# A macaron layer on one core: the work between the last mixed chunk and the first paired chunks, in another order and other banks

## The reference

```python
x = x + 0.5 * ffn(layernorm(x)); x = x + mixer(layernorm(x)); x = x + 0.5 * ffn(layernorm(x))
# ffn: x = fwht(x * SU_ug) / 64;  h = silu(x @ W_gate.T * s1) * (x @ W_up.T * s2)
#      fwht(h * SU_dp) / 64 @ W_down.T * s3                      (512 -> 2048 -> 512)
# mixer: y = ssd(...) * silu(gate); y = y * rsqrt(mean(y*y) + eps) * norm_w; y @ out_proj_w.T
```

## Time and profile before

| what | value |
|---|---|
| runs | 1649.05 us median of 3 (1648.89 to 1649.43) |
| the profiled execution | 1650.64 us, its span 1648.9 us |
| busy | TensorE 98%, VectorE 66%, ScalarE 40%, GpSimd 28% of the span |
| mean granted clock of TensorE | 0.995 |

### The profile page before, as it was taken

The page is one execution under the profiler, slowest core; times in us unless marked ns, Lnnn a source line. Parts: engine busy times, 40 slices in busy tenths (PEclk is TensorE's granted clock), DMA queues, the critical chain, the costliest instruction groups (busy, mean ns, idle before and its releaser), DMA issues.

```text
span 1648.9 us, 25148 instructions
## 1 busy us (share of the span) xinstructions
PE 1615.0 (98%) x9612; PEld 1304.5 (79%) x9612; DVE 1087.8 (66%) x2096; ACT 660.8 (40%) x988; POOL 459.6 (28%) x365
## 2 busy tenths in 40 slices
PE   7999999999999999999999999999999999899999
PEld 4788888878888778888778888877888877678887
DVE  7544445675677777777776768777775775665543
ACT  5334343464433463333454333355333341343321
POOL 1666662012212212212212222222131221543400
PEclk9999999999999999999999999999999999999999
DMA  7855555654454444454444444445444435432334
GB/s 285 303 201 206 215 192 204 230 182 153 159 167 163 137 160 152 152 171 144 154 163 149 157 165 152 158 146 183 146 166 162 161 106 178 141 128 90 128 101 155
DMA packets 230886, 274.76 MB, mean 167 GB/s; under 512 B 14064, under 2 KB 190320, under 8 KB 222192
## 3 DMA queue, kind: packets, MB, share of 16 engines
q1 hardware_dynamic: 230768, 273.15, 49.3%
HBM read 222.79 MB, written 50.33 MB: 166 GB/s over the span
## 4 chain that ended last, share of the span: by engine, by line
PE 69%; DVE 5%; ACT 2%; issue 2%; DMA 1%; POOL 1%; SPq 0%; ACTq 0%; DVEq 0%; POOLq 0%
PE bank L1263 23%; PE bank L1219 12%; PE bank L1306 10%; PE bank L1431 5%; PE bank L1343 5%; PE bank L1320 3%; PE bank L1500 3%; PE bank L1471 2%; PE bank L1487 2%; PE bank L1449 2%; PE bank L1494 1%; PE bank L1459 1%; DMA cum_stay<-m_aS 1%; DVE res L2044 1%; DVE xT L2018 0%
## 5 line engine op out<-in xcount | busy, mean ns | idle before, releaser
L1263 PE MATMUL bank<-fxT,wj 128*128 128x512 f32 x1608 | 381.5, 390 | 0.0
L1263 PEld LDWEIGHTS bank<-fxT,wj 128*128 128x128 f32 x1608 | 301.6, 188 | 62.8
L1219 PE MATMUL bank<-xT,wi 128*128 128x512 f32 x900 | 225.8, 399 | 1.5 <-DVE m_cv L2127 0.5
L1306 PE MATMUL bank<-m_wd,m_hb 128*128 128x512 f32 x864 | 218.0, 395 | 3.6 <-DVE res L2044 2.7
L1219 PEld LDWEIGHTS bank<-xT,wi 128*128 128x128 f32 x900 | 168.2, 190 | 40.3 <-issue 5.0
L1306 PEld LDWEIGHTS bank<-m_wd,m_hb 128*128 128x128 f32 x864 | 161.1, 189 | 37.9 <-DVE res L2044 3.8
L1734 ACT CAST m_hb<-xn 128x512 fp32r<-128x512 f32 x76 | 47.1, 620 | 342.8 <-DVE xn L2031 334.9
L2492 POOL TENSOR_TENSOR m_L<-m_L,m_GT 128x512 f32<-128x512 f32 x36 | 52.7, 1463 | 436.7 <-ACT m_L L1788 436.7
L2044 DVE TENSOR_TENSOR res<-bank,res 128x512 f32<-128x512 f32 x148 | 101.9, 689 | 34.6 <-PE bank L1306 32.5
L1788 ACT ACTIVATE m_L<-bank 128x512 f32<-128x512 f32 x128 | 76.5, 598 | 86.8 <-PE bank L1449 86.5
L2031 DVE SCALAR_TENSOR_TENSOR xn<-bank,sc,xn 128x512 f32<-128x512 f32 x76 | 56.7, 746 | 68.1 <-PE bank L1263 68.0
(11 more groups left out here) (279 smaller groups left out, 2742.0 us busy)
## 6 DMA issues: line engine op xcount, KB each, us to landing
wj<-ug_split SPq DMA_DIRECT2D x155, 512.0 KB, 4.2
m_wd<-dn_split SPq DMA_DIRECT2D x43, 1024.0 KB, 4.9
wi<-in_split SPq DMA_DIRECT2D x76, 512.0 KB, 3.3
ug_split<-b_wu SPq DMA_DIRECT2D x8, 2048.0 KB, 14.2
m_wo<-out_split SPq DMA_DIRECT2D x32, 512.0 KB, 4.1
in_split<-b_msp SPq DMA_DIRECT2D x20, 512.0 KB, 3.8
wi<-ug_split SPq DMA_DIRECT2D x17, 512.0 KB, 4.2
raw<-in_wug SPq DMA_DIRECT2D x8, 1024.0 KB, 6.9
```

Of the source, the lines that this page charges most:

```text
L1219: ins = pe.matmul(to[:], w[:, a, k, :], xT[:, b, k, :], start=(k == 0 and i == 0), stop=(k == KH - 1 and i == 2))
L1263: ins = pe.matmul(to[:], w[:, a, k, :], frm[:, b, k, :], start=(k == 0 and i == 0), stop=(k == KH - 1 and i == 2))
L1306: ins = pe.matmul(F[t % 2][:], hb[:, a, j, ck(t)], w[:, b, j, :], start=(j == 0 and n == 0), stop=(j == 1 and n == 2))
```

## The change

- The last output projection writes its four groups to banks 1, 3, 2 and 5 (`last_out_bank`) instead of 6 and 7 in turn, and waits for the last readers of those banks.
- The down product of chunk 33 writes to banks 6, 7, 0 and 1 (`down_bank`), and the gate and up products of chunk 34 wait for two additions less.
- On VectorE the small operations of the root stand behind the four additions of chunk 32's down product, instead of ahead of them.
- On TensorE the turns of the last sequence stand behind chunk 33's second up product; ScalarE and VectorE follow.
- Sums of rows 2 and 3 and the low part of 2 are made by VectorE (`third_difference`, `fourth_difference`, `sums_of_rows_low`); GpSimd keeps `sums_of_weights`. The low parts of all four are done before the first unit, in the order 1, 0, 2, 3 (`SPLIT`), and ScalarE rounds all four ahead of the hidden rows of chunk 34.

```diff
     PRODUCTS = 7
+    SPLIT = (1, 0, 2, 3)
+    SUMMED = (TPG, TPG, TPG + 1, TPG + 4)
+    SPLIT_UP = (TPG + 3, TPG + 2, TPG + 5, TPG + 6)
     order = [BI_DT, BI_B, BI_C] + [i for b in range(NB) for i in (NB + b, b)]
...
 
+        def down_bank(at, t):
+
+            return (F[0], F[1], PB, A)[t] if at == MIXED + 1 else F[t % 2]
+
+        def last_out_bank(t):
+
+            return (A, X, Y, S[1])[t]
+
         def ending_bank(t):
...
                 if x == 0:
-                    sp.wait_ge(s_tp, TPG + 2)
+                    sp.wait_ge(s_tv, SUMMED[3])
                 elif x <= PAIRED + 1:
...
 
-            def up0(at, pairs=0):
-                wait(pe, s_acc, downs(at) - 1)
-                wait(pe, s_oa, TPG * pairs)
+            def up0(at):
+                wait(pe, s_acc, downs(at) - (3 if at == MIXED + 2 else 1))
                 half_up(4 * place_of(at) + 1, F[0]).then_inc(s_u, 1)
...
                 if not opens(at):
-                    pe.wait_ge(s_acc, downs(at))
+                    pe.wait_ge(s_acc, downs(at) - (2 if at == MIXED + 2 else 0))
                 pe.wait_ge(s_sil, 2 * at + 1)
...
                     pe.wait_ge(s_sil, 2 * at + 2 if closes(at) else 2 * at + 3)
-                else:
+                elif at != MIXED + 1:
                     pe.wait_ge(s_acc, downs(at) + t - 1)
+                elif t == 2:
+                    pe.wait_ge(s_pev, LGATE * BATCH)
+                else:
+                    pe.wait_ge(s_oa, TPG * NPAIR * BATCH)
                 for j in range(2):
                     for n, (a, b) in enumerate(PASSES):
-                        ins = pe.matmul(F[t % 2][:], hb[:, a, j, ck(t)], w[:, b, j, :], start=(j == 0 and n == 0), stop=(j == 1 and n == 2))
+                        ins = pe.matmul(down_bank(at, t)[:], hb[:, a, j, ck(t)], w[:, b, j, :], start=(j == 0 and n == 0), stop=(j == 1 and n == 2))
                 ins.then_inc(s_d, 1)
...
                 else:
-                    pe.wait_ge(s_L, QUADS * MIXED)
+                    pe.wait_ge(s_acc, TPG * (MIXED + 2))
                 product(x_bank, a11, b11, True)
...
                 pe.wait_ge(s_sl, u + 1)
-                pe.wait_ge(s_tv, TPG + 2)
+                pe.wait_ge(s_tv, SPLIT_UP[1])
                 pe.wait_ge(s_sn, 4 * u + 1)
...
                 pe.wait_ge(s_cc, 3 * u + 1)
+                pe.wait_ge(s_tv, SPLIT_UP[0])
                 product(y_bank, s1, t1, True)
                 part(1 if u else 3)
-                pe.wait_ge(s_tp, TPG + 3)
+                pe.wait_ge(s_tv, SPLIT_UP[2])
                 pe.wait_ge(s_sn, 4 * u + 2)
...
                 pe.wait_ge(u_loaded, u_count)
-                pe.wait_ge(s_tv, TPG + 3)
+                pe.wait_ge(s_tv, SPLIT_UP[3])
                 pe.wait_ge(s_sn, 4 * u + 4)
...
                 pe.wait_ge(s_yl, 2 * (pair + 1))
+                if pair == NPAIR * BATCH - 1:
+                    pe.wait_ge(s_L, QUADS * MIXED)
+                    pe.wait_ge(s_ex, MIXED)
+                    pe.wait_ge(s_y, MIXED)
+                    pe.wait_ge(s_st, MIXED)
                 for t in range(TPG):
-                    if t >= 2:
+                    if pair == NPAIR * BATCH - 1:
+                        to = last_out_bank(t)
+                    else:
+                        to = F[1 - t % 2]
+                    if pair == NPAIR * BATCH - 1:
+                        pass
+                    elif t >= 2:
                         pe.wait_ge(s_oa, TPG * pair + t - 1)
-                    elif pair == NPAIR * BATCH - 1:
-                        pe.wait_ge(s_acc, downs(at) - t)
                     elif t == 0:
...
                         for n, (a, b) in enumerate(PASSES):
-                            ins = pe.matmul(F[1 - t % 2][:], yh[:, (2 * pair + i) % 4, a, ck(t)], wout[i][:, b, :],
+                            ins = pe.matmul(to[:], yh[:, (2 * pair + i) % 4, a, ck(t)], wout[i][:, b, :],
                                             start=(i == 0 and n == 0), stop=(i == 1 and n == 2))
...
                     out_proj(NPAIR * BATCH - 1, at)
-                up0(at, NPAIR * BATCH if at == MIXED else 0)
+                up0(at)
                 gate1(at)
-                if at == MIXED + SOLO - 2:
+                up1(at)
+                if at == MIXED + 1:
                     for t in range(TPG):
                         beside_turn(ITEMS - 1, t)
-                up1(at)
                 if at < MIXED + SOLO - 1:
...
                 else:
-                    act.wait_ge(s_tv, TPG + 3)
-                    act.wait_ge(s_tp, TPG + 3)
+                    act.wait_ge(s_tv, SPLIT_UP[3])
                 act.copy(pair_hidden(p, g)[:, 0, j, :], four(u)[:, g, :]).then_inc(s_hh, 1)
...
 
-                if i < 2:
-                    act.wait_ge(s_tv, TPG)
-                else:
-                    act.wait_ge(s_tp, TPG + i - 1)
+                act.wait_ge(s_tv, SUMMED[i])
                 act.copy(tb[:, 0, i], tf[:, i]).then_inc(s_th, 1)
...
             hidden_high(at, 0)
+            silu(at, 1)
             for t in range(TPG):
                 beside_row(ITEMS - 1, t)
-            silu(at, 1)
             for t in range(TPG):
...
             silu(at, 0)
-            sums_of_rows_high(0)
-            sums_of_rows_high(1)
-            sums_of_rows_high(2)
+            for i in SPLIT:
+                sums_of_rows_high(i)
             hidden_high(at, 0)
-            silu(at, 1)
             sums_of_weights_high(0)
+            silu(at, 1)
             hidden_high(at, 1)
...
                 paired_silu(u, 0)
-                if u == 0:
-                    sums_of_rows_high(3)
                 snapshot(u, 3, 4, y_bank)
...
                 dve.wait_ge(s_d, downs(at) + t + 1)
-                frm = end_bank(t) if at == LAST - 1 else F[t % 2]
+                frm = end_bank(t) if at == LAST - 1 else down_bank(at, t)
                 dve.tensor_tensor(r, frm[:], r, ALU.add).then_inc(s_acc, 1)
...
 
+            def third_difference():
+                dve.wait_ge(s_tv, TPG)
+                dve.tensor_tensor(tf[:, 2], tf[:, 1], bf[:, 0:2], ALU.subtract).then_inc(s_tv, 1)
+
+            def fourth_difference():
+                dve.wait_ge(s_tv, TPG)
+                dve.tensor_tensor(tf[:, 3], bf[:, 2:4], tf[:, 1], ALU.subtract).then_inc(s_tv, 1)
+
             def sums_of_rows_low(i):
 
-                dve.wait_ge(s_th, i + 1)
+                dve.wait_ge(s_th, 1 + SPLIT.index(i))
                 dve.tensor_tensor(tb[:, 1, i], tf[:, i], tb[:, 0, i].bitcast(F32), ALU.subtract).then_inc(s_tv, 1)
...
                 dve.wait_ge(s_op, TPG * pair + t + 1)
+                frm = last_out_bank(t) if pair == NPAIR * BATCH - 1 else F[1 - t % 2]
                 if pair % NPAIR:
-                    dve.tensor_tensor(acc[:, t, :], F[1 - t % 2][:], acc[:, t, :], ALU.add).then_inc(s_oa, 1)
+                    dve.tensor_tensor(acc[:, t, :], frm[:], acc[:, t, :], ALU.add).then_inc(s_oa, 1)
                 else:
-                    dve.tensor_copy(acc[:, t, :], F[1 - t % 2][:]).then_inc(s_oa, 1)
+                    dve.tensor_copy(acc[:, t, :], frm[:]).then_inc(s_oa, 1)
 
...
             next(other)
-            next(other)
             at = MIXED + 1
...
             next(other)
-            bias(1, s_fs)
             hidden(at, 0)
+            next(other)
+            bias(1, s_fs)
             hidden_low(at, 0)
+            hidden(at, 1)
             for t in range(TPG):
                 beside_turn(ITEMS - 1, t)
-            row_differences(0)
-            hidden(at, 1)
             hidden_low(at, 1)
-            at = MIXED + 2
             for t in range(TPG):
-                add_down(at - 1, t)
-                if t < TPG - 1:
-                    row_differences(t + 1)
-            sums_of_rows_low(0)
+                row_differences(t)
+            at = MIXED + 2
+            add_down(at - 1, 0)
+            add_down(at - 1, 1)
+            third_difference()
+            add_down(at - 1, 2)
             sums_of_rows_low(1)
+            add_down(at - 1, 3)
+            sums_of_rows_low(0)
+            fourth_difference()
             hidden(at, 0)
             hidden_low(at, 0)
-            hidden(at, 1)
+            sums_of_rows_low(2)
+            sums_of_rows_low(3)
             sums_of_weights_low(0)
+            hidden(at, 1)
             hidden_low(at, 1)
...
                     part(3)
-                    sums_of_rows_low(3)
                 second_up(u)
...
                 pool.tensor_tensor(bf[:, k], xT[:, 0, k].bitcast(F32), xT[:, 1, k].bitcast(F32), ALU.add).then_inc(s_tp, 1)
-            pool.wait_ge(s_tp, TPG)
-            pool.wait_ge(s_tv, TPG)
-            pool.tensor_tensor(tf[:, 2], tf[:, 1], bf[:, 0:2], ALU.subtract).then_inc(s_tp, 1)
-            sums_of_weights(0)
-            pool.tensor_tensor(tf[:, 3], bf[:, 2:4], tf[:, 1], ALU.subtract).then_inc(s_tp, 1)
-            pool.wait_ge(s_th, 3)
```

(3 more changed lines are left out.)

20 lines of the change are left out of this document (10 added, 10 removed).

## The result

The changed kernel took 1634.95 us (median of 4 runs, 1634.84 to 1636.11) against 1649.24 us of the kernel before (median of 4, 1648.89 to 1650.29): a ratio of 0.9914, 95% interval 0.9897 to 0.9931. The forecast was 1638.0 us in a range from 1636.0 to 1642.5. Two more comparisons of the same two kernels, each on one chip, gave 0.9929 (0.9917 to 0.9941) and 0.9933 (0.9920 to 0.9946); the forecast was 1638.0 / 1649.05 = 0.9933.

What follows compares the result with a forecast made beforehand. TensorE, busy 98%, was the bound; only its standing and low clock, 16.0 us, could go. Gains 1.08 - 0.5 + 4.2 + 1.1 + 0.15 + 3.1 + 2.2 = 11.3, less 0.3, took 1649.05 to 1638.0; range 1636.0 to 1642.5.

Steps and rivals of the forecast that it cites:

- The time outside the stretch: Outside last output projection to first pair of chunks nothing is touched; profiled 1650.64 us would become about 1639.6, median 1638.0.
- Start of chunk 32's down product: TensorE stands 1.1 us instead of 0.61, waiting for VectorE's second low part of the hidden rows: a loss of 0.5.
- the better rival: Chunk 32's low part slips through (0.5 us) and the VectorE-GpSimd blocks vanish (1.5): gain 13.0, time 1636.0; chance 8%.
- the third down group's stall and its slow clock: In chunk 32's down product, roots moved behind the down additions leave standing of 0.1 us and no low clock: gain 4.2.
- the turns: Moved behind chunk 33's second up product, they wait for nothing; chunk 33's down product starts 5.99 us earlier, gain 1.1.
- the last stall: Ahead of chunk 34's down product TensorE stands 1.9 us where 5.02 were too many: gain 3.1.
- The blocks between VectorE and GpSimd: Ahead of chunk 34's second up product they alternate by whole operations; that product stands 1.45 us, gain 0.15.
- The full clock behind the two stalls: After stalls of 1.45 and 1.9 us around chunk 34, no low clock follows; 2.20 us of low clock goes.
- The output projection's banks: No bank shared with the next up product, which starts at 1378.63 without waiting for the last accumulation: gain 1.08 us.
- VectorE as the bound: Rival: GpSimd operations block VectorE in full (3.9 us) and the low clock costs 2.2: gain 4.9, time 1644; chance 11%.
- the kept low clock: Slower rival: the lower clock stays after the stalls at 1421.6 and 1429; 150 slow multiplications would give 1665 us; chance 3%.
- The missed turn: Rival: the last low part waits 1.3 us behind GpSimd, chunk 34's down product stalls 3.2: gain 8.2, time 1640.8; chance 22%.

Runs made afterwards that it cites:

- banks_only: The kernel before with only the four banks for the last output projection and their waits: ratio 1.0005 (0.9995 to 1.0014) of the kernel before, median 1648.51 us.

## Why the forecast was wrong, step by step

**The time outside the stretch.** The step that failed is "the profiled execution took 1650.64 (span 1648.9) and would come to about 1639.6; the median shown is 1649.05, so the median comes to **1638.0**", with "Nothing else in the program is touched, so this is the ceiling". It took the 1373.18 us ahead of the change as fixed. They are not: they lie between 1368.56 and 1373.18 in fourteen traces, and the trace of before happened to have the longest. Three runs within 0.5 us of each other didn't show it. The profiled execution came out 3.5 us below its forecast of 1639.6 (1636.11): 2.32 of this is the head, 1.2 the stretch (12.2 gained, 11.0 forecast). A gain of 12.2 alone would have given about 1637, inside the range. The medians, 14.3 apart, have no traces of their own, but the rest behind the stretch repeats within 0.16 us, so what goes beyond the stretch's 11.7 to 12.2 can only lie in the head. The range had no term for it.

**Start of chunk 32's down product.** The forecast took the low part there at its blocked 1.29 and put the other case, 0.5 more, into the better rival. It took 0.69 in all three traces of the change, and in banks_only too: 0.26 gained instead of 0.5 lost, 0.76. From there on every start is 0.5 to 0.8 sooner than forecast: chunk 34's down product stood 55.77 us behind the projection's start in the working (1428.95 - 1373.18) and came at 55.00. The allowance of 0.3 for hand-overs wasn't needed.

**Right in mechanism and size** (the table under the result): the third down group's stall and its slow clock (4.2 forecast, 4.15), the turns (1.1, 1.32), and the last stall (1.9 forecast, 7.31 - 5.45 = 1.86).

**Right in part by luck.** The blocks between VectorE and GpSimd came by turns, as forecast, but not where forecast. The working had the third difference run free in 1.22 and GpSimd begin behind it; GpSimd began 0.07 ahead, and the difference took 2.32. Later blocks fell away for it, so the hidden product still ended about where the sum had it: forecast 48.4 us behind the projection's start, 1418.50 - 1370.86 = 47.6 measured, with the start of the chain 0.7 sooner. The full clock behind the two stalls (1.00 and 1.55) held in all three traces of the change. The forecast took it from the length of the stall alone, and the head shows that this isn't enough: there an idle time of 1.40 in the changed kernel was followed by a clock of 0.67 (355.80 to 361.00), and one of 0.54 by twelve slow multiplications in five traces of fourteen.

**The output projection's banks** gained 0.95 in the change, as forecast (1.08), but not by themselves: the roots had to move too (banks_only).

**The sums of rows** on VectorE are worth 2.0 us, three quarters of it in the twelve multiplications behind the last stall.

**The rivals.** VectorE as the bound and the kept low clock didn't occur. The missed turn didn't either, but by little: the last low part began at 1424.91, when GpSimd's first sum for the second unit (1423.71 and 1.30 long) had 0.1 us to go, and so was ahead of the second. The "better" case with its slip of 0.5 did occur in part, and with the head's chance it gave the time.

In the second and third comparisons, with 23 and 17 runs of the kernel before and 5 and 6 of the changed one, 11.5 and 12.5 us were gained against 11.0 forecast.

## What to carry to other kernels

Where two engines exchange work by turns, move whatever has slack (a root, a low part that is needed later) behind what releases the waiting engine, and price a stall of TensorE with the slow multiplications that follow it. Two edits that each shorten one wait may need each other: test them alone and together before giving either a value. And cut every trace in head, changed stretch and rest: the stretch repeated within 0.02 us here for the changed kernel and 0.55 for the one before, while whole executions spread over several.
